# Perceiver block: normalizing attention outputs two head groups at a time, with the softmax sums copied beside them by DMA

## The chip, the cores and the metric

One NeuronCore of one Trainium2 chip runs the whole program. The metric is the device time of one execution in microseconds (us). All times below come from timed runs or from one profiled execution.

## The reference, cut to what matters

The input is `x` (4 batches of 256 tokens, width 256) and a context of 4096 rows of width 192 for each batch. All is float32.

```python
x = x + xattn(layernorm(x), ctx)      # 16 heads of 16; 256 queries, 4096 keys per batch
x = x + attn(layernorm(x))            # 16 heads; keys within 32 positions of the query
x = x + ffn(layernorm(x))             # 16 banks of 256 -> 1024 -> 256, the best 2 of each token
# in both attentions, per head:
out = softmax(q @ k.T / 4) @ v        # then all heads side by side, @ w_out + b_out
```

The softmax is computed as `exp(score - max)`, weighed with `[v, 1]`, and divided by its sum only afterwards. That last division, and how its operands reach their places, is what is changed.

## The kernel before

**Cross-attention (first stage).** Heads go in groups of four (`GH`), so 4 batches give `GROUPS = 16` groups. Each group has `KT = 32` steps, one for 128 keys; there are `STEPS = 512` steps. In step n TensorE (PE) computes the scores of the step (`scores`, L721), the products from which the row maxima of a step 36 later are taken (`max_pair`, L691), and the weighing of an earlier step (`weigh`, L739). ScalarE (ACT) takes the exponential of each step (`empty`, L1242). VectorE (DVE) takes two maxima from PSUM a step (`max_one`, L1494). Between these lie side jobs, written out by `side_jobs(n)`: keys ("kk"), values ("v"), the maxima as rows ("neg"), "norm" and "out". Each side job takes its turn on two pairs of PSUM banks with the scores (`bank_pair`).

`weigh` leaves in PSUM, for head j of the group, rows 32j to 32j+15 of output and row 32j+16 with the softmax sum. ACT copies the 128 x 256 tile to `o_raw` (`ocopy`, L1289). The job "norm", at step 6 of the next group, is a PE matmul of `o_raw` with the selector `lsel` (L747), which puts each head's sum on its rows. ACT copies the result to `total` (L1278), DVE makes a first guess of 1/total by its bits (`guess`, L1517, at step 8), and GpSimd (POOL) refines it three times and multiplies it onto `o_raw` (`norm`, L2040 to L2048). `close_up` (SyncE's queue, SP, at step 17, `CLOSE_AT`) then copies the 16 rows of each head into `o_close`, 128 rows without gaps, by four DMAs. After four groups "out" projects `o_close` (L754, step 22). So there are 15 norm jobs in the loop. The last group is normalized after the loop by `last_norm`: a matmul (L985), a DVE reciprocal (L1523), a product and a sum on DVE.

**Windowed attention (second stage).** Its 16 `PAIRS` run in a PE order written by hand, for i = 1 to 15: `max2(i,0)`, `neg2(i-1)`, `weigh2(i-2,0)`, `scores2(i-1)`, `max2(i,1)`, `weigh2(i-2,1)`, `norm2(i-3)`. After i = 3 follows `last_project` (L900); after i = 5, 6 and 7 the second half of rows, queries, keys and values (`turn_half`, `qk_half`, `v_tile2`), each behind a wait for the exponentials of pair i-1; after i = 8 and 12 `project2` (L880). `norm2` is again an `lsel` matmul (L867); ACT copies its result (`sums2`, L1343), DVE takes the reciprocal (`reciprocals2`, L1554), and POOL multiplies and adds the bias (`norm2`, L2127, L2129). `close_up` again follows. `neg2`, `norm2`, the projections and the logits share one PSUM bank, in the order of `x_uses()`.

**After it.** Routing, then the banks' products on 24 tiles, with 31 loads of weights by DMA. Neither is touched.

Of the kernel before, what the change touches and what calls it, by code (L numbers as in the profile page):

```python
# [16 lines left out]
P = 128  # L17
# [71 lines left out]
CLOSE_AT = 17  # L89
# [68 lines left out]
def side_jobs(n):  # L158
# [38 lines left out]
def weighing():  # L197

    plan, waiting = {}, []
    for n in range(STEPS + 2):  # L200
# [3 lines left out]
        put_off = n < STEPS and len(waiting) < 2 and kinds & {"kk", "v"} and not (kinds & {"neg", "norm"} or after & {"kk", "v"})  # L204
# [18 lines left out]
def x_uses():  # L223

    order = ["norm"]
    for i in range(1, PAIRS):
        order += [("neg2", i - 1)]
        order += [("norm2", i - 3)] if i >= 3 else []
        order += ["out"] if i == 3 else []
        order += [("out2", (i - 8) // NG)] if i in (8, 12) else []  # L230
    order += [("neg2", PAIRS - 1), ("norm2", PAIRS - 3), "logits"]
    return {use: n for n, use in enumerate(order)}
# [24 lines left out]
def build(nc, a, out, scratch):  # L257
    ctx = ExitStack()
    with ctx:
# [8 lines left out]
        def bank(i, n=1):  # L268
# [15 lines left out]
        o_norm = sp_all.tile("o_norm", (NG, SEQ))  # L284
        o_close = sp_all.tile("o_close", (KE, SEQ))
        kept = sp_all.at
# [12 lines left out]
        vals = s1.tile("vals", (KT, HEADS * VW))  # L299
        wts_at = s1.at  # L300
# [13 lines left out]
        total = s1.tile("total", (SEQ,))  # L314
# [10 lines left out]
        bv = s1.tile("bv", (NG,))  # L325
# [49 lines left out]
        bv2 = s2.tile("bv2", (NG,))  # L375
        bo2 = s2.tile("bo2", (EMB,))
        q2 = s2.tile("q2", (2, KE, TOK))
        vals2 = s2.tile("vals2", (TT, HEADS * VW))
        wmask = s2.tile("wmask", (2, WIN))
# [16 lines left out]
        sum2 = [s2.tile(f"sum2_{i}", (SEQ,)) for i in range(2)]  # L396

# [57 lines left out]
        st_qk, pool_lo, ld_o = semaphores("st_qk", "pool_lo", "ld_o")  # L455
# [13 lines left out]
        pe_lastnorm, dve_lastnorm, pe_lastout, dve_lastx = semaphores(  # L469
            "pe_lastnorm", "dve_lastnorm", "pe_lastout", "dve_lastx")  # L470
# [39 lines left out]
        def closed(g):  # L510

            return 16 * GH * (g + 1)
# [38 lines left out]
        def _(e):  # L551
# [216 lines left out]
            def side_job(job):  # L768
# [6 lines left out]
                elif job[0] == "norm":  # L775
                    norm(job[1])
# [98 lines left out]
            def project2(b):  # L875
                e.wait_ge(ld_o, closed(GROUPS + NG * b + NG - 1))
                e.wait_ge(x_free, X_NO["out2", b])
                for qt in range(BT):
                    for k in range(KE):
                        i = e.matmul(bank(X_BANK)[:, qt * EMB:(qt + 1) * EMB], o_close[:, k, qt * P:(qt + 1) * P],  # L880
# [3 lines left out]
            def project_third(qt):  # L884

                if qt == 0:
                    e.wait_ge(ld_o, closed(GROUPS + NG * (BATCH - 1) - 1))
                    e.wait_ge(dve_m2, 2 * PAIRS)
                for k in range(KE):
                    i = e.matmul(bank(W_BANKS[qt])[:, 0:EMB], o_close[:, k, qt * P:(qt + 1) * P], wo2[:, k],  # L890
# [3 lines left out]
            def last_project():  # L894

                e.wait_ge(ld_o, closed(LAST))
# [34 lines left out]
            def early(j):  # L931
                dst = bank(M_BANKS[j % 2])
                if j == 0:
                    e.wait_ge(ld_b, 16 * 8)
# [27 lines left out]
            for n in range(-LEAD, STEPS + 2):  # L962
# [13 lines left out]
                for job in jobs:  # L976
                    if job[0] in ("neg", "norm", "out"):
                        side_job(job)
# [5 lines left out]
            e.wait_ge(act_ocopy, GROUPS)  # L984
            e.matmul(bank(X_BANK)[:, 0:SEQ], lsel, o_raw, start=True, stop=True).then_inc(pe_lastnorm, 1)  # L985
# [33 lines left out]
            for i in range(1, PAIRS):  # L1019
                max2(i, 0)  # L1020
                neg2(i - 1)
                if i >= 2:
                    weigh2(i - 2, 0)
                scores2(i - 1)
                max2(i, 1)
                if i >= 2:
                    weigh2(i - 2, 1)
                if i >= 3:
# [15 lines left out]
                if i in (8, 12):  # L1044
                    project2((i - 8) // NG)
# [1419 lines left out]
```

## Time and profile before

| what | value |
|---|---|
| median of 3 runs | 1208.67 us (1207.93 to 1208.95) |
| profiled execution, its own time | 1209.17 us |
| its span, first to last instruction | 1207.4 us |
| mean granted TensorE clock | 0.986 |
| PE, DVE, ACT, POOL busy | 97%, 71%, 59%, 35% of the span |
| first stage, steps 0 to 511 | 78.6 to about 850.3 us |
| second stage | about 850.3 to about 978 us |

The profiled execution's own time lies 1.8 us over its span and 0.5 us over the median of the runs. Times in the rows are us from the start of the span. Busy time of PE is modelled, so a busy PE is not PE at its peak; what a job costs is read from the distance between the starts of its neighbours.

### The profile page before, as it was taken

How to read it: one execution, taken by the hardware profiler on the slowest of the kernel's cores; microseconds unless marked ns; L12 is line 12 of the kernel's file. 1: busy time of each engine (PE TensorE's matmuls, PEld its weight loads, DVE VectorE, ACT ScalarE, POOL GpSimd, SP SyncE). 2: the span in 40 equal slices, each digit the busy share in tenths (PEclk: the TensorE clock that was granted, in tenths of full speed). 3: DMA queues.
4: the chain of work that ended last, by engine and by line, in shares of the span. 5: the costliest groups of instructions: out<-in, count | busy, mean ns of one | idle time of the engine just before them, and what ended most of it. 6: DMA issues, size and time to landing. Idle time of an engine off the chain costs nothing.

```text
span 1207.4 us, 29836 instructions
## 1 busy us (share of the span) xinstructions
PE 1174.8 (97%) x12106; PEld 721.4 (60%) x12106; DVE 862.5 (71%) x1663; ACT 714.8 (59%) x923; POOL 425.4 (35%) x429
## 2 busy tenths in 40 slices
PE   8989999999999999999999999999899979999998
PEld 5555454566545566655456654444556568778787
DVE  4987899977899987789988789962375774233234
ACT  4437778877787877788777778895233310121120
POOL 3385593225462333554332312212022423222210
PEclk9989999999999999999999999999899998999999
DMA  8766756554575465465644455220300009999993
GB/s 235 111 154 179 188 109 155 122 118 121 129 173 121 110 140 146 122 143 116 148 106 91 102 121 113 56 64 4 89 8 10 11 38 351 413 413 396 390 392 114
DMA packets 62648, 184.78 MB, mean 153 GB/s; under 512 B 19888, under 2 KB 27824, under 8 KB 54576
## 3 DMA queue, kind: packets, MB, share of 16 engines
q1 hardware_dynamic: 58352, 171.27, 51.1%
q0 software_dynamic: 2432, 7.11, 1.8%
q10 hardware_dynamic: 1728, 4.49, 1.0%
q8 instruction: 96, 1.57, 0.6%
q14 instruction: 40, 0.33, 0.1%
HBM read 138.20 MB, written 39.58 MB: 147 GB/s over the span
## 4 chain that ended last, share of the span: by engine, by line
PE 88%; DVE 4%; ACT 2%; DMA 2%; issue 1%; SPq 1%; POOL 1%; ACTq 0%; DVEq 0%; POOLq 0%
PE psum L739 22%; PE psum L721 17%; PE psum L691 10%; PE psum L1152 5%; PE psum L1180 5%; PE psum L589 5%; PE psum L605 4%; PE psum L1177 2%; PE psum L1146 2%; PE psum L802 2%; DVE part_max L1484 1%; ACT wts L1242 1%; PE psum L921 1%; PE psum L796 1%; PE psum L622 1%
## 5 line engine op out<-in xcount | busy, mean ns | idle before, releaser
L1494 DVE TENSOR_REDUCE part_max<-psum 128x1 f32<-128x512 f32 x952 | 600.1, 686 | 98.4 <-PE psum L691 96.7
L1242 ACT ACTIVATE wts<-psum 128x1024 f32<-128x1024 f32 x512 | 518.7, 1024 | 99.4 <-PE psum L721 97.9
L739 PE MATMUL psum<-wts,vals 128*17 128x256 f32 x4096 | 307.2, 384 | 0.5 <-ACT o_raw L1289 0.5
L721 PEld LDWEIGHTS psum<-queries,keys 51*128 51x128 f32 x2048 | 155.8, 185 | 186.3 <-issue 149.6
L721 PE MATMUL psum<-queries,keys 51*128 51x256 f32 x2048 | 255.3, 327 | 2.1 <-ACT queries L1274 0.2
L691 PE MATMUL psum<-keys,queries 51*128 51x512 f32 x1024 | 219.1, 411 | 6.7 <-DVE part_max L1484 2.8
L739 PEld LDWEIGHTS psum<-wts,vals 128*17 128x17 f32 x4096 | 75.1, 96 | 118.7 <-issue 90.3
L691 PEld LDWEIGHTS psum<-keys,queries 51*128 51x128 f32 x1024 | 110.5, 186 | 22.3 <-DVE part_max L1484 10.8
L2040 POOL TENSOR_TENSOR error<-total,o_norm 128x256 f32<-128x256 f32 x45 | 33.0, 734 | 205.8 <-DVE o_norm L1517 203.4
L1414 ACT ACTIVATE hid<-psum,b1s 128x128 f32<-128x128 f32 (+1 forms) x124 | 31.7, 351 | 113.7 <-PE psum L1152 77.3
L1973 POOL CAST key_high<-key_low 128x1024 fp32r<-128x1024 f32 x28 | 29.0, 1036 | 178.0 <-ACT key_low L1255 178.0
L2177 POOL DMA_INDIRECT rows_y<-yout,to_row x22 | 21.7, 987 | 130.0 <-DVE yout L1904 130.0
L1975 POOL TENSOR_TENSOR key_low<-key_low,key_high 128x1024 fp32r<-128x1024 f32 x28 | 66.6, 2380 | 2.3
L1152 PE MATMUL psum<-xTt,w1s 128*128 128x128 f32 x544 | 63.6, 276 | 0.2 <-issue 0.2
L1895 DVE TENSOR_SCALAR hid<-psum,b1s 128x128 f32<-128x128 f32 (+1 forms) x124 | 30.5, 313 | 45.5 <-PE psum L1152 42.4
L1152 PEld LDWEIGHTS psum<-xTt,w1s 128*128 128x128 f32 x544 | 62.2, 192 | 0.5 <-issue 0.4
L1180 PE MATMUL psum<-w2s,hid 128*128 128x256 f32 x272 | 62.1, 382 | 0.0
L1180 PEld LDWEIGHTS psum<-w2s,hid 128*128 128x128 f32 x272 | 50.5, 190 | 11.8 <-issue 5.7
L1988 POOL TENSOR_TENSOR ctx_lo<-ctx_in,ctx_hi 128x1536 fp32r<-128x1536 f32 x16 | 55.7, 3480 | 1.3
L1261 ACT ACTIVATE vals<-psum 128x512 f32<-128x512 f32 x64 | 38.2, 599 | 29.7 <-PE psum L605 16.6
L1533 DVE TENSOR_REDUCE neg_max<-psum 128x4 f32<-128x640 f32 x32 | 26.4, 824 | 38.3 <-PE psum L802 38.3
L1255 ACT ACTIVATE key_low<-psum,bk_two 128x1024 f32<-128x1024 f32 x28 | 31.2, 1115 | 37.4 <-PE psum L589 37.4
(281 smaller groups left out, 1494.1 us busy)
## 6 DMA issues: line engine op xcount, KB each, us to landing
w1s<-in_W SPq DMA_DIRECT2D x31, 1024.0 KB, 10.7
w2s<-in_W SPq DMA_DIRECT2D x31, 1024.0 KB, 11.7
keys<-k_high SPq DMA_DIRECT2D x232, 128.0 KB, 3.9
keys<-k_low SPq DMA_DIRECT2D x116, 128.0 KB, 4.5
k_high<-key_high SPq DMA_DIRECT2D x28, 512.0 KB, 4.9
k_low<-key_low SPq DMA_DIRECT2D x28, 512.0 KB, 3.8
ctx_in<-in_ctxT SPq DMA_DIRECT2D x12, 768.0 KB, 6.5
ctx_in<-in_ctxT ACTq DMA_DIRECT2D x4, 768.0 KB, 12.3
```

The lines of the kernel that those rows point to most:

```text
L589: t = e.matmul(bank(first + odd), w[rows, r, hp * P:(hp + 1) * P], c[rows, p, r * CH:(r + 1) * CH], start=(r == 0 and n == 0), stop=(r == ...
L605: m = e.matmul(bank(first + odd)[:, 0:EMB], c[rows, p, at:at + P], w[rows, r], start=(r == 0 and n == 0), stop=(r == CB - 1 and n == 2))
L691: e.matmul(bank(LEAD_BANKS[m % 2] + i if m < LEAD else M_BANKS[(2 * m + i) % 3]), queries[g % 3][64 * i:64 * i + STK, hh, qt * P:(qt + 1) ...
L721: m = e.matmul(bank(S_BANKS[S_NO["s", n] % 2] + i)[:, hh * SEQ:(hh + 1) * SEQ], keys[64 * i:64 * i + STK, hh, c, at:at + P], queries[g % 3 ...
L739: i = e.matmul(bank(O_BANK)[32 * j:32 * j + VW, 0:SEQ], vals[:, t, h * VW:(h + 1) * VW], wts[n % NW][:, j * SEQ:(j + 1) * SEQ], start=(t = ...
L1152: i = e.matmul(dst[:, q * P:(q + 1) * P], w1s[w[0]][:, k, hc * P:(hc + 1) * P], xTt[j % 2][:, k], start=(k == 0), stop=(k == KE - 1))
L1180: i = e.matmul(dst, hid[j % 2][:, hc], w2s[w[0]][:, hc], start=(hc == 0), stop=(hc == HC - 1))
L1242: i = e.activation(wts[n % NW], s_bank(job, 2), ACT.Exp, scale=QSCALE)
L1261: i = e.activation(vals[:, t:last + 1:CH // P].rearrange("p t (h w) -> p t h w", w=VW)[:, :, :, 0:HD], s_bank(job, 2).rearrange("p (t h w) ...
L1494: e.reduce_max(part_max[g % 2][:, hq, c:c + 1], bank(M_BANKS[n % 3]), AX_X).then_inc(dve_max, 1)
L1975: e.tensor_tensor(key_low, key_f, key_high.bitcast(F32), ALU.subtract).then_inc(split_low, 1)
L1988: e.tensor_tensor(ctx_lo[:, p], ctx_in[:, p], ctx_hi[:, p].bitcast(F32), ALU.subtract).then_inc(pool_lo, 1)
```

## The change

1. The "norm" jobs, `last_norm`, and the `lsel` matmuls of the second stage's first 12 pairs (`WIDE`) are gone, with their ACT copies.
2. `close_up` now copies from the raw outputs, right after ACT has made them (step 2 of the next group): four DMAs for the heads' rows and a fifth one that reads the four rows of sums and writes each 16 times, into `total`, beside the rows it belongs to.
3. Two groups fill the 128 rows of `total` and of one half of `o_close`. DVE's guess and POOL's refinement then run once for two groups, in place on `o_close`, at step 14 (`INVERSE_AT`) of every second group. "out" moves from step 22 to 24. The eighth of these (groups 14 and 15) lies in the second stage.
4. `ocopy` waits for the DMAs of the group before instead of for POOL's product. The weights of the second stage (`ld_b`) are nine loads instead of eight and stand behind `close_up(14)` on SP's queue.
5. The second stage has tiles of its own (`o_close2`, `total2`, `inverse2`). DVE takes one reciprocal for two pairs (`inverse_two`), between its two maxima of i = 5, 7, ... 15. The PE order becomes `max2(i,0)`, `project2`, `neg2(i-1)`, `weigh2(i-2,0)`, `weigh2(i-2,1)`, `max2(i,1)`, `scores2(i-1)`. The last batch's pairs 12 to 15 keep the `lsel` matmuls.

```diff
-CLOSE_AT = 17
+CLOSE_AT, INVERSE_AT = 2, 14
+WIDE = NG * (BATCH - 1)
...
-    if at == 6 and 0 <= g < LAST:
-        jobs.append(("norm", g))
-    if at == 22 and hg == NG - 1 and 0 <= b < BATCH - 1:
+    if at == 24 and hg == NG - 1 and 0 <= b < BATCH - 1:
         jobs.append(("out", b))
...
 # TensorE
-            def norm(g):
-                bank_pair(("norm", g))
-                e.wait_ge(act_ocopy, g + 1)
-                e.matmul(s_bank(("norm", g))[:, 0:SEQ], lsel, o_raw, start=True, stop=True).then_inc(pe_s, 1)
...
             def project(b):
-                e.wait_ge(ld_o, closed(NG * b + NG - 1))
+                e.wait_ge(pool_norm, KE * (b + 1))
...
             def last_project():
-                e.wait_ge(ld_o, closed(LAST))
+                e.wait_ge(pool_norm, GROUPS // 2)
...
-            e.wait_ge(act_ocopy, GROUPS)
-            e.matmul(bank(X_BANK)[:, 0:SEQ], lsel, o_raw, start=True, stop=True).then_inc(pe_lastnorm, 1)
...
             for i in range(1, PAIRS):
                 max2(i, 0)
+                if i in (8, 12):
+                    project2((i - 8) // NG)
                 neg2(i - 1)
                 if i >= 2:
                     weigh2(i - 2, 0)
+                    weigh2(i - 2, 1)
+                max2(i, 1)
                 scores2(i - 1)
-                max2(i, 1)
-                if i >= 2:
-                    weigh2(i - 2, 1)
-                if i >= 3:
+                if i - 3 >= WIDE:
                     norm2(i - 3)
...
 # ScalarE
             def ocopy(g):
                 if g:
-                    e.wait_ge(pool_omul, g)
+                    e.wait_ge(ld_o[(g - 1) % 2], closed(g - 1))
...
             def ocopy2(p):
-                if 1 < p < PAIRS - 1:
-                    e.wait_ge(pool_omul2, p - 1)
+                if 1 < p < WIDE + 2:
+                    e.wait_ge(ld_o[p % 2], closed(GROUPS + p - 2))
+                elif p == WIDE + 2:
+                    e.wait_ge(pool_omul2, inverted(p - 2))
...
                 neg_rows(i - 1)
-                exps(i - 1)
                 if i >= 2:
                     ocopy2(i - 2)
-                if i >= 3:
+                exps(i - 1)
+                if i - 3 >= WIDE:
                     sums2(i - 3)
...
 # VectorE
+            def guess(u):
+                if u:
+                    e.wait_ge(pool_norm, u)
+                for i in range(2):
+                    e.wait_ge(ld_o[i], closed(2 * u + i))
+                e.tensor_scalar(inverse.bitcast(I32), total.bitcast(I32), -1.0, INVERSE_BITS, ALU.mult, ALU.add).then_inc(dve_guess, 1)
...
+            def inverse_two(u):
+                if u:
+                    e.wait_ge(pool_omul2, u)
+                for i in range(2):
+                    e.wait_ge(ld_o[i], closed(GROUPS + 2 * u + i))
+                e.reciprocal(inverse2, total2[u % 2]).then_inc(dve_rec2, 1)
...
-                if n >= KT and n % KT == 8:
-                    guess(n // KT - 1)
+                if n % (2 * KT) == INVERSE_AT and n >= KT:
+                    guess(n // (2 * KT) - 1)
...
                 max2(i, 0)
-                if i >= 4:
-                    reciprocals2(i - 4)
+                if i >= 5 and i % 2:
+                    inverse_two((i - 5) // 2)
+                if i in (8, 12):
+                    add_out2((i - 8) // NG)
                 max2(i, 1)
                 pieces2(i)
+                if i == 1:
+                    guess(GROUPS // 2 - 1)
...
 # GpSimd
+            def norm(u):
+                o = o_close[:, u % KE]
+                e.wait_ge(dve_guess, u + 1)
+                for _ in range(3):
+                    e.tensor_tensor(error, total, inverse, ALU.mult)
+                    e.tensor_scalar(error, error, -1.0, 2.0, ALU.mult, ALU.add)
+                    e.tensor_tensor(inverse, inverse, error, ALU.mult)
+                e.tensor_tensor(o, o, inverse, ALU.mult).then_inc(pool_omul, 1)
+                e.tensor_scalar_add(o, o, bv[:, u % KE:u % KE + 1]).then_inc(pool_norm, 1)
...
+            def norm_two(u):
+                o = o_close2[u // KE % 2][:, u % KE]
+                e.wait_ge(dve_rec2, u + 1)
+                e.tensor_tensor(o, o, inverse2, ALU.mult).then_inc(pool_omul2, 1)
+                e.tensor_scalar_add(o, o, bv2[:, u % KE:u % KE + 1]).then_inc(pool_norm2, 1)
...
 # SyncE's DMA queue
-            def close_up(g):
+            def close_up(g, raw, dst, beside):
                 hg = g % NG
-                if g:
-                    e.wait_ge(ld_o, closed(g - 1))
+                if g > 1:
+                    e.wait_ge(ld_o[g % 2], closed(g - 2))
+                rows = slice(64 * (hg % 2), 64 * (hg % 2) + 64)
                 for j in range(GH):
-                    at = 64 * (hg % 2) + HD * j
-                    e.dma_start(o_close[at:at + HD, hg // 2], o_norm[32 * j:32 * j + HD, hg]).then_inc(ld_o, 16)
+                    e.dma_start(dst[rows.start + HD * j:rows.start + HD * (j + 1), hg // 2],
+                                raw[32 * j:32 * j + HD]).then_inc(ld_o[g % 2], 16)
+                e.dma_start(beside[rows], raw[HD::32].rearrange("p (o t) -> p o t", o=1).broadcast_to([GH, HD, SEQ])).then_inc(ld_o[g % 2], 16)
```

## Rows read from the trace of the kernel before

**Rows 1.** The page: busy us, share of the span and instructions of each engine.
```profile
PE 1174.8 (97%) x12106; PEld 721.4 (60%) x12106; DVE 862.5 (71%) x1663; ACT 714.8 (59%) x923; POOL 425.4 (35%) x429
```
**Rows 2.** Groups of instructions: busy us, mean ns of one, idle before and its releaser.
```profile
L747 PE MATMUL psum<-o_raw,lsel 128*128 128x256 f32 x30 | 10.5, 432 | 0.0
L1517 DVE TENSOR_SCALAR o_norm<-total 128x256 int32<-128x256 int32 x15 | 4.3, 285 | 2.3 <-PE psum L721 2.3
L1554 DVE RECIPROCAL sum<-sum 128x256 f32<-128x256 f32 x14 | 24.4, 1744 | 0.4 <-ACT sum L1343 0.4
```
**Rows 3.** Timeline of PE around one norm job: start us, length us.
```profile
337.31 0.51 PE L721 MATMUL psum<-queries,keys 51*128 51x256 f32 x4
339.19 0.50 PE L721 MATMUL psum<-queries,keys 51*128 51x256 f32 x4
340.41 0.51 PE L721 MATMUL psum<-queries,keys 51*128 51x256 f32 x4
```
**Rows 4.** Timeline of DVE over the same steps.
```profile
339.95 2.51 DVE L1494 TENSOR_REDUCE part_max<-psum 128x1 f32<-128x512 f32 x4 [0.58 <-PE psum L691]
```
**Rows 5.** Timelines of SP's queue and of PE: second stage's loads, their first user.
```profile
799.93 0.34 SPq L2309 DMA_DIRECT2D wqkv<-in_w_qkv  x1
...
815.52 0.66 PE L916 MATMUL psum<-identf,xn 128*128 128x128 f32 x4
```
**Rows 6.** The tile o_close: ns of one issue (min/median/max), us from issue to landing.
```profile
L2259 SPq DMA_DIRECT2D o_close<-o_norm x112: 507/589/1612, 163.0 to 968.0; - x112
...
DMA to landing us min/median/max: 1.7/2.3/4.4
```
**Rows 7.** The chain of waits across the hand-over to the second stage.
```profile
849.32 1.03 PE psum L739 x16
...
851.61 1.77 DVE o_norm L1523
853.52 0.27 PE psum L811 x2
```
**Rows 8.** Windows: length, busy PE, PEld, DVE, ACT, POOL, then PEclk.
```profile
853.70:857.20 3.50, 3.50 (x36) 2.16 (x33) 1.22 (x3) 1.04 (x3) 0.00 (x0) 0.52 0.28 48
...
945.00:982.00 37.00, 31.64 (x371) 20.48 (x370) 29.13 (x67) 10.84 (x23) 14.88 (x19) 1.00 0.07 23
```
**Rows 9.** Timeline of all engines, one iteration (i = 10) of the second stage.
```profile
925.28 0.31 PE L796 MATMUL psum<-wmaskb,identb 128*128 128x160 bf16 x2
926.71 0.29 PE L811 MATMUL psum<-identb,neg_parts 128*128 128x128 bf16 x2
927.33 0.72 PE L830 MATMUL psum<-wmaskb,identb 128*128 128x320 bf16 x4
928.87 0.31 PE L796 MATMUL psum<-wmaskb,identb 128*128 128x160 bf16 x2
928.98 1.30 ACT L1336 ACTIVATE wT<-psum 128x640 f32<-128x640 f32 x2 [1.56 <-PE psum L843]
930.41 0.82 DVE L1533 TENSOR_REDUCE neg_max<-psum 128x4 f32<-128x640 f32 x1 [1.11 <-PE psum L802]
930.70 0.70 PE L867 MATMUL psum<-o_raw,lsel 128*128 128x256 f32 x2
931.29 0.31 PE L796 MATMUL psum<-wmaskb,identb 128*128 128x160 bf16 x2
```
**Rows 10.** Timeline of the second stage: where blocks start, and the last waits.
```profile
873.27 1.10 PE L900 MATMUL psum<-wo,o_close 128*128 128x256 f32 x4 [0.57 <-ACT sum L1343]
...
919.27 0.30 PE L796 MATMUL psum<-wmaskb,identb 128*128 128x160 bf16 x2
...
937.31 0.31 PE L796 MATMUL psum<-wmaskb,identb 128*128 128x160 bf16 x2
...
969.88 1.13 PE L890 MATMUL psum<-wo,o_close 128*128 128x256 f32 x4 [1.71 <-DMA o_close<-o_norm]
...
971.90 1.75 DVE L1554 RECIPROCAL sum<-sum 128x256 f32<-128x256 f32 x1 [0.35 <-ACT sum L1343]
```

More of the change, by code:

```diff
@@ L203, in weighing @@
         after = {job[0] for job in side_jobs(n + 1)} if n + 1 < STEPS else set()
-        put_off = n < STEPS and len(waiting) < 2 and kinds & {"kk", "v"} and not (kinds & {"neg", "norm"} or after & {"kk", "v"})
+        put_off = n < STEPS and len(waiting) < 2 and kinds & {"kk", "v"} and not ("neg" in kinds or after & {"kk", "v"})
         plan[n] = [] if put_off else waiting
@@ L223, in x_uses @@
 def x_uses():
-    order = ["norm"]
+    order = []
     for i in range(1, PAIRS):
+        order += [("out2", (i - 8) // NG)] if i in (8, 12) else []
         order += [("neg2", i - 1)]
-        order += [("norm2", i - 3)] if i >= 3 else []
+        order += [("norm2", i - 3)] if i - 3 >= WIDE else []
         order += ["out"] if i == 3 else []
-        order += [("out2", (i - 8) // NG)] if i in (8, 12) else []
     order += [("neg2", PAIRS - 1), ("norm2", PAIRS - 3), "logits"]
@@ L454, in build @@
         ld_duo = [semaphore(f"ld_duo{i}") for i in range(2)]
-        st_qk, pool_lo, ld_o = semaphores("st_qk", "pool_lo", "ld_o")
+        st_qk, pool_lo = semaphores("st_qk", "pool_lo")
+        ld_o = [semaphore(f"ld_o{i}") for i in range(2)]
         ld_first, pe_first, act_first, dve_firsth, dve_firstl, pool_identb = semaphores(
@@ L976, in _ @@
                 for job in jobs:
-                    if job[0] in ("neg", "norm", "out"):
+                    if job[0] in ("neg", "out"):
                         side_job(job)
@@ L1274, in empty @@
                         i = e.activation(q[at:at + NP].rearrange("p h t -> p (h t)"), src[at:at + NP], ACT.Copy)
-                elif kind == "norm":
-                    if job[1]:
-                        e.wait_ge(pool_omul, job[1])
-                    i = e.activation(total, src[:, 0:SEQ], ACT.Copy)
                 else:
@@ L1302, in _ @@
             e.wait_ge(ld_const, 16)
-            e.activation(total[:, 0:P], identf, ACT.Exp)
+            e.activation(inverse[:, 0:P], identf, ACT.Exp)
             key_ones(slot(4))
@@ L1509, in max_end @@
                 e.wait_ge(dve_negp, g + 1)
-            def guess(g):
-                b, hg = divmod(g, NG)
-                if b:
-                    e.wait_ge(pe_s, done(("out", b - 1)))
-                e.wait_ge(act_s, done(("norm", g)))
-                e.tensor_scalar(o_norm[:, hg].bitcast(I32), total.bitcast(I32), -1.0, INVERSE_BITS, ALU.mult, ALU.add).then_inc(dve_guess, 1)
-            def last_norm():
-                e.wait_ge(pe_s, done(("out", BATCH - 2)))
-                e.wait_ge(pe_lastnorm, 1)
-                e.reciprocal(o_norm[:, NG - 1], bank(X_BANK)[:, 0:SEQ]).then_inc(x_free, 1)
-                e.wait_ge(x_free, X_NO["norm"] + 1)
-                e.tensor_tensor(o_norm[:, NG - 1], o_raw, o_norm[:, NG - 1], ALU.mult).then_inc(own.up(), 1)
-                e.wait_ge(dve_seq, own.n)
-                e.tensor_scalar_add(o_norm[:, NG - 1], o_norm[:, NG - 1], bv[:, NG - 1:NG]).then_inc(dve_lastnorm, 1)
+            def guess(u):
[4 more added lines that the diff above has]
+                e.tensor_scalar(inverse.bitcast(I32), total.bitcast(I32), -1.0, INVERSE_BITS, ALU.mult, ALU.add).then_inc(dve_guess, 1)
             def max2(p, qt):
@@ L1674, in _ @@
             pieces2(0)
-            last_norm()
             last = range((BATCH - 1) * BT, TT)
@@ L2140, in _ @@
                                         ALU.subtract, ALU.mult).then_inc(pool_rows3, 1)
+            for p in range(WIDE, PAIRS - 1):
+                norm2(p)
             for t in (tiles, ends[0], ends[1]):
@@ L2299, in _ @@
                     load_q(e, n // KT + 2)
-                if KT <= n < LAST * KT and n % KT == CLOSE_AT:
-                    e.wait_ge(pool_norm, n // KT)
-                    close_up(n // KT - 1)
+                if n >= KT and n % KT == CLOSE_AT:
+                    g = n // KT - 1
+                    e.wait_ge(act_ocopy, g + 1)
+                    if g > 1 and g % 2 == 0:
+                        e.wait_ge(pool_norm, g // 2)
+                    if g and g % NG == 0:
+                        e.wait_ge(pe_s, done(("out", g // NG - 1)))
+                    close_up(g, o_raw, o_close, total)
             e.wait_ge(pe_s, S_NO["s", LAST * KT])
```

138 lines of the change are left out of this document (65 added, 73 removed).

## The prediction

> **What bounds the kernel now.** I read the page first, then the groups of instructions, then timelines of PE and DVE in the loop and over the second stage, and last the windows with the granted clock. The page shows PE busy for 97% of the span and DVE for 71% [rows 1]. In the loop's plain steps both are full: DVE's maxima follow each other every 2.51 / 4 = 0.63 us, which is 1.26 us for the two of a step [rows 4], and PE's steps start 1.22 to 1.26 us apart [rows 3]. They are tied to each other, for a maximum must leave its bank before PE fills it again. What a step holds beside that lengthens it, and DVE cannot run ahead. The step with the norm job shows this: its scores start at 337.31 and the next ones at 339.19, 1.88 us [rows 3], and DVE then stands idle for 0.58 us [rows 4].
>
> In the second stage PE sets the pace with short waits for DVE and ACT. One iteration takes 931.29 - 925.28 = 6.01 us [rows 9]. By the starts in it `max2` takes 1.43 us, `neg2` and a half of `weigh2` 0.62 (0.22 and 0.40), `scores2` 1.54, `norm2` 0.59. The reader is to see that `norm2` ends at about the time when DVE's maximum does (930.41 + 0.82 = 931.23), and PE's next block waits for that maximum: to take `norm2` out in the old order would give nothing, PE would wait there instead. The new order puts `scores2` behind `max2(i,1)`, so it is the order that makes the gain possible.
>
> **The loop.** 15 norm jobs, two matmul records each [rows 2], stand in it. Each costs 1.88 - 1.26 = 0.62 us of PE's path, so 15 x 0.62 = 9.3 us go. (Busy time alone would say 2 x 432 ns; the starts say what counts.) ACT's copies for them lie inside these 0.62 us. DVE's guess takes 0.285 us [rows 2] and costs something only where DVE is full: eight of the 15 stood in groups without values jobs, four of the new seven do. That is 4 fewer at between 0 and 0.285 us, so 0 to 1.1; I take 0.5. POOL's chain runs half as often, but POOL is busy 35% of the span [rows 1] and its results had slack, so I count nothing; if the cover were gone, a late chain would hold "out". The chain is nine operations and two more, 8 us, started at step 14; "out" at step 24 comes at least 12.5 us later.
>
> What is queued behind the new waits? SP's `close_up` at step 2 stands behind 14 issues of that region (`load_duo` six, `load_q` six, `store_two` two). At 0.589 us each [rows 6] it begins 8.2 us after step 0, its five issues end at 11.2, and at the worst landing of 4.4 us [rows 6] all is there at 15.6. DVE's guess at step 14 comes 14 x 1.26 = 17.6 us after step 0 at the earliest, and keys jobs add to that. The slack of 2 us covers the wait; without it DVE's maxima behind the guess, and so PE, would lose whatever is late. The next `load_duo` (step 8) starts 1 to 2 us late, but its keys are used 12 steps later.
>
> One DMA batch gets later where it shows. The second stage's loads began at 799.93 and their first user on PE ran at 815.52 [rows 5]. Now `close_up(14)` stands before them. It waits for ACT's copy at step 481, about 803.4, and issues five times: the loads begin at 806.4 and are nine. In the old trace data moved for 7.6 us from the first issue, so they land at about 814.0 to 814.5. The user comes at 815.52 - 0.62 = 814.9. So 0 to 2 us are lost; I take 0.3. The loop gives 9.3 + 0.5 - 0.3 = 9.5 us.
>
> **The second stage, up to `last_project`.** The old hand-over: PE ends weighing at 850.35, `last_norm` holds the shared bank, `neg2(0)` starts at 853.52 [rows 7], and PE's clock then stands at 0.52 of full speed for about 3.4 us, and once more at 860.5 [rows 8]. `last_project` starts at 873.27 [rows 10], 22.9 us after the weighing. New: i = 1 is two `max2`, `neg2`, `scores2` and a wait of 0.78 for DVE's first maximum, 5.4 us; i = 2 and 3 are 2 x 1.43 + 0.22 + 2 x 0.40 + 1.54 = 5.42 us each. Sum 16.2 us, so 6.7 us gained; about 3 of them are the clock. `last_project` then starts at about 866.6 in old times. It needs the eighth chain on POOL: five issues from 850.8, landing at about 856.2, then 0.3 of guess and 8 us of POOL, 864.6. DVE waits for that landing in front of the maximum that PE needs at 858.2, so each us of landing past 857 is a us lost; I take 0.3 off.
>
> A rule speaks against the fifth DMA. Its source begins with the four sum rows. The trace of before holds no copy of this shape. The Trainium skill (DMA: Bandwidth & Descriptors, "Why a DMA increments its semaphore by 16 and not by 1") says that a copy uses the largest number of engines up to 16 that divides both slowest dimensions, so this one would run on four, with 16 KB each. At that page's 436 GB/s for all 16 it is an estimate of 0.6 us more, and the sum would be 16.5 instead of 17.1 if all of it came onto PE's path.
>
> **From there to i = 8.** Old: 873.27 to 919.27 [rows 10], 46.0 us. Each of i = 4 to 8 loses 6.01 - 5.42 = 0.59, together 3.0 us. But `scores2` now ends the iteration, and after i = 5, 6, 7 PE waits for both exponentials of that very pair before the second half's blocks. These take 0.11 + 1.30 + 0.05 us from the end of `scores2` [rows 9]; the old order had 2.4 us of other PE work there. This is a new wait of 1.46 us, three times: 4.4 us lost. At i = 4 and 5 DVE's statistics and root stand before the maxima: 0.4 and 0.75 us more than before. At i = 8 `neg2` waits 0.87 for DVE to empty the projection, and 0.56 of waiting for `sums2` goes. Net 3.0 - 4.4 - 1.15 - 0.3 = -2.9 us.
>
> **The rest.** i = 9 to 11: 3 x 0.59 = 1.8 us gained. i = 12 to DVE's last `L1554` reciprocal, 937.31 to 971.90 [rows 10], 34.6 us: new i = 12 is 5.42 + 1.80 + 0.87 = 8.1, i = 13 and 14 are 6.2 each with waits of 0.8 for DVE (statistics, root), and from i = 15 to that reciprocal 11.4 us, since PE's waits for POOL's product and for the last copies, 1.71 us [rows 10], go: 31.9, 2.7 us gained. DVE's reciprocals fall from 14 to 8 of 1.74 us [rows 2]; that lies beside PE and is what keeps the waits this small. Stage two: 6.7 - 0.3 - 2.9 + 1.8 + 2.7 = 8.0; by bounds 3 to 11. I take 7.6, since each wait was placed with exact starts and some will be worse.
>
> Routing and the banks' products only move. Sum: 9.5 + 7.6 = 17.1 us. The profiled execution of 1209.17 becomes 1192.1; it lay 0.5 above the median, so the runs should show 1191.6.
>
> **Rivals.** *The clock stays low in the second stage.* The old drops came behind short waits; the new ones (0.78, and 1.46 three times) are of the size of those at 965 to 970, where the clock stayed full [rows 8]. If two stretches of 3.4 us at half speed come as before, 3.4 us are lost: 1195.0. Chance 0.25. *DVE, not PE, is the loop's pace,* and the norm step's 0.62 us were caught up later: then only 8 us come back, 1201. Against it: DVE idled, and the next steps of 1.22 are no shorter than the others [rows 3, 4]. Chance 0.08. *Slower: the sums land late.* Place: DVE's wait in `guess` and `inverse_two`, 14 of them, with all maxima queued behind. It decides from a landing of about 2 us past my worst of 4.4; each further us costs 7 in the loop and up to 7 later, so at 3.2 us past it the gain is gone, and at 4 the time is near 1218. For it: keys' loads share the queue at step 8. Against it: 112 copies never took over 4.4 [rows 6]. Chance 0.05. *The new waits of the second stage are larger* (exponentials, DVE's order, loads at 814): 3 to 5 us, 1195.5. Chance 0.10. My forecast has the remaining 0.52, between 1189 and 1194.
>
> **Range.** 1187.5 to 1198.5 holds the forecast and the clock and wait cases, and leaves out the caught-up loop, the late landing and an end that is better than all bounds. No change that this kernel's measurement can tell is within 0.2%, 2.4 us. Faster 0.93, same 0.02, slower 0.05.
>
> **What the new profile would show.** No 1.88 us step at step 6 of a group; plain steps still 1.22 to 1.28. The first stage ends near 841, 9.5 us earlier. No `L985`-like matmul and no half clock behind it. In iterations 9 to 11 starts 5.4 us apart. Three PE waits of about 1.5 us for ACT's exponentials before the transposes, the queries' products and the values'. DVE's guesses with no wait for DMA in front. I am wrong if DVE waits on the sums' copies, if the steps grow elsewhere, or if half clock comes back.

## The result and the profile after

Four runs of the changed kernel have a median of 1197.64 us (1187.7 to 1201.35), against 1208.81 us for the kernel before: a ratio of 0.9891 (95% interval 0.9853 to 0.9928). The kernel is faster by 11 us where 17 were forecast. The profiled execution took 1196.13 us (span 1194.3), at a mean granted TensorE clock of 0.986, the same as before (1.00 is 2.4 GHz and 0.50 is 1.2 GHz, the two levels that occur).

The page's first line (busy us, share of the span, instructions) answers [rows 1]:

```profile
PE 1156.3 (97%) x12050; PEld 712.7 (60%) x12050; DVE 848.6 (71%) x1647; ACT 704.9 (59%) x896; POOL 365.4 (31%) x340
```

The first stage first: the timeline of PE at steps 4 to 8 of group 5, to be laid beside [rows 3].

```profile
328.68 0.50 PE L731 MATMUL psum<-queries,keys 51*128 51x256 f32 x4
329.91 0.50 PE L731 MATMUL psum<-queries,keys 51*128 51x256 f32 x4
331.17 0.50 PE L731 MATMUL psum<-queries,keys 51*128 51x256 f32 x4
332.41 0.50 PE L731 MATMUL psum<-queries,keys 51*128 51x256 f32 x4
333.66 0.50 PE L731 MATMUL psum<-queries,keys 51*128 51x256 f32 x4
```

The 1.88 us step is gone: 331.17 to 332.41 is 1.24. The plain steps around it are what they were. From step 0 to the end of weighing the loop took 838.47 - 75.3 = 763.2 us, against 850.35 - 78.6 = 771.75 before: 8.6 us less. (Another 3.3 us came from ahead of step 0. In the old profile PE waits 2.35 us at 29.63 there, and half clock comes at 31; by the same product of keys and queries, 37.80 before and 35.64 now, 2.2 us are there already. Ten further profiles of the changed kernel and its variants start step 0 at 75.2 to 76.5. With one profile of the kernel before, it is not shown whether any of this belongs to the change.)

Then the second stage. The timeline of PE, only blocks with a wait in front, and the two starts that frame i = 4 to 8 (856.44 and 911.77):

```profile
840.84 0.31 PE L798 MATMUL psum<-wmaskb,identb 128*128 128x160 bf16 x2 [0.71 <-DVE neg_max L1518]
...
854.61 1.99 PE L902 MATMUL psum<-wo,o_close 128*128 128x256 f32 x8
856.44 0.30 PE L798 MATMUL psum<-wmaskb,identb 128*128 128x160 bf16 x2
...
859.53 0.31 PE L798 MATMUL psum<-wmaskb,identb 128*128 128x160 bf16 x2 [0.71 <-DVE neg_max L1518]
...
866.22 0.31 PE L798 MATMUL psum<-wmaskb,identb 128*128 128x160 bf16 x2 [1.33 <-DVE neg_max L1518]
866.47 0.54 PE L804 MATMUL psum<-k,q 32*128 32x160 f32 x4
866.94 0.31 PE L798 MATMUL psum<-wmaskb,identb 128*128 128x160 bf16 x2
867.18 0.90 PE L804 MATMUL psum<-k,q 32*128 32x160 f32 x4
...
872.30 1.97 PE L918 MATMUL psum<-identf,xn 128*128 128x128 f32 x8 [1.39 <-ACT wT L1333]
...
884.76 8.56 PE L923 MATMUL psum<-xT,wqkv 128*128 128x512 f32 x16 [1.39 <-ACT wT L1333]
...
900.00 3.72 PE L929 MATMUL psum<-wqkv,xT 128*128 128x256 f32 x16 [1.39 <-ACT wT L1333]
907.92 0.27 PE L813 MATMUL psum<-identb,neg_parts 128*128 128x128 bf16 x2 [0.94 <-DVE x L1576]
...
911.77 0.31 PE L798 MATMUL psum<-wmaskb,identb 128*128 128x160 bf16 x2
...
914.20 0.31 PE L798 MATMUL psum<-wmaskb,identb 128*128 128x160 bf16 x2
...
919.60 0.31 PE L798 MATMUL psum<-wmaskb,identb 128*128 128x160 bf16 x2
```

`last_project` starts 854.61 - 838.47 = 16.1 us after the weighing, where it was 22.9. The iterations from i = 9 on are 919.60 - 914.20 = 5.40 us, where one took 6.01 [rows 9]. The three blocks of the second half each wait 1.39 us for ACT's exponentials. Ahead of them stand waits of 0.71 and 1.33 us for DVE's maxima, at i = 4 and 5. Behind the second of these the same product of keys and queries takes 0.54 us at 866.47 and 0.90 us at 867.18: the clock has fallen, 5 us before the first wait for exponentials ends. The windows (columns as in [rows 8]) show for how long:

```profile
838.50:866.00 27.50, 24.90 (x334) 15.53 (x333) 16.06 (x49) 9.03 (x18) 7.70 (x13) 1.00 0.40 114
866.00:890.00 24.00, 20.99 (x135) 12.00 (x136) 7.88 (x16) 4.56 (x8) 3.02 (x4) 0.57 0.05 12
890.00:945.00 55.00, 50.52 (x624) 31.64 (x622) 30.27 (x71) 18.02 (x36) 7.07 (x9) 1.00 0.07 18
945.00:966.00 21.00, 18.57 (x225) 12.28 (x226) 14.68 (x22) 6.49 (x14) 11.32 (x15) 1.00 0.07 27
```

A mean of 0.57 over 24 us is 24 x 0.43 / 0.5 = 20.6 us at 1.2 GHz, in one piece. At the hand-over, where the old kernel fell to half clock twice, this one stays at 2.4 GHz. So from 856.44 to 911.77 PE needs 55.3 us, where the old kernel needed 919.27 - 875.08 = 44.2 for the same iterations with their `norm2`. What the hand-over and the shorter iterations gave, 6.8 us and 0.6 each, is gone again in this one place: from the end of weighing to the first late reciprocal (961.32) the second stage takes 122.9 us, and took 973.6 - 850.35 = 123.25 before.

Last, SP and DVE at the eighth guess, the only one of 14 uses of the copied sums that waited for its DMA (four copies of rows go ahead of that of the sums):

```profile
838.95 3.04 SPq L2261 DMA_DIRECT2D o_close<-o_raw  x4
842.03 0.60 SPq L2263 DMA_DIRECT2D total<-o_raw  x1
...
845.08 0.29 DVE L1512 TENSOR_SCALAR inverse<-total 128x256 int32<-128x256 int32 x1 [0.99 <-DMA total<-o_raw]
```

### The profile page after: what moved, and what is told of

Its sections match the earlier page's. It is cut to its first block, busy times and chain, and to the rows that moved or that the text cites. A ratio compares the mean times of both kernels' runs of the same rounds, so it can differ in the third digit from the quotient of the medians.

```text
span 1194.3 us, 29561 instructions
## 1 busy us (share of the span) xinstructions
PE 1156.3 (97%) x12050; PEld 712.7 (60%) x12050; DVE 848.6 (71%) x1647; ACT 704.9 (59%) x896; POOL 365.4 (31%) x340
## 3 DMA queue, kind: packets, MB, share of 16 engines
q8 instruction: 96, 1.57, 0.6%
## 4 chain that ended last, share of the span: by engine, by line
PE 84%; DVE 8%; ACT 3%; issue 2%; DMA 1%; SPq 1%; ACTq 0%; POOL 0%; DVEq 0%; POOLq 0%
PE psum L749 20%; PE psum L731 16%; PE psum L701 10%; PE psum L1151 5%; PE psum L1179 5%; PE psum L599 5%; PE psum L615 4%; DVE part_max L1489 3%; PE psum L804 2%; PE psum L1176 2%; PE psum L1145 2%; DVE part_max L1479 1%; PE psum L923 1%; ACT wts L1241 1%; PE psum L798 1%
## 5 line engine op out<-in xcount | busy, mean ns | idle before, releaser
L1409 ACT ACTIVATE hid<-psum,b1s 128x128 f32<-128x128 f32 (+1 forms) x124 | 31.7, 351 | 113.2 <-PE psum L1151 76.8
L1898 DVE COPY yout<-psum 128x256 f32<-128x256 f32 x22 | 9.3, 425 | 56.7 <-PE psum L1179 39.3
```

## The experiments

Ten runs of eight kernels were made in three groups; those of a group shared a chip and its runs of the kernel before. Diffs are against the changed kernel. Each line of the table gives its median over all its executions. The last two columns come from one fit over all 145 executions whose clock is known: one level for each kernel, one slope for all; the changed kernel's level rests on its first four executions too. The slope is 0.99 us (standard error 0.02) for each 0.001 of mean granted clock. "Against the changed kernel" is then the difference in work and waits at one clock, with its 95% bound.

| kernel | executions | median us | ratio to before | mean clock | at clock 0.985, against the changed kernel |
|---|---|---|---|---|---|
| before | 57 | 1210.35 | | 0.985 | +13.9 ± 0.6 |
| changed: again, again2 | 12, 12 | 1203.03, 1199.38 | 0.9954, 0.9912 | 0.978, 0.980 | 0 (level 1195.9) |
| later | 6 | 1194.51 | 0.9869 | 0.983 | -4.0 ± 1.1 |
| fill | 6 | 1190.65 | 0.9878 | 0.989 | +1.0 ± 1.2 |
| oldorder | 12 | 1200.45 | 0.9941 | 0.977 | -1.1 ± 0.8 |
| dummy | 12 | 1211.52 | 1.003 | 0.979 | +10.1 ± 0.8 |
| loads | 6 | 1196.14 | 0.9882 | 0.985 | 0.0 ± 1.1 |
| both | 6 | 1187.95 | 0.9814 | 0.988 | -4.9 ± 1.2 |
| best, best2 | 6, 6 | 1186.4, 1184.18 | 0.9802, 0.9773 | 0.990, 0.992 | -4.8 ± 1.0 |

**again: the changed kernel untouched, for its spread.**

> The changed kernel itself, run more often. Its four runs so far lie between 1187.7 and 1201.35 us with mean granted clocks of 0.991 and 0.980. Theory (the clock): the time falls in line with the mean granted clock, run by run; with 0.990 and more about 1188, with 0.980 about 1201, and the profile of a slow one shows a long stretch of about half clock in the second stage that a fast one lacks. Rival (something else varies, such as DMA landings in the loop): times and clocks are not in line, and the profile shows longer steps in the first stage.

It took 1203.03 us (1193.68 to 1213.72), 0.9954 of before (0.9917 to 0.999). The profile is the first one over again: all three exponential waits, and half clock at the same place for the same time. The first stage is as long (762.6 us, was 763.2), and times and clocks are in line, so the rival falls. Windows:

```profile
838.50:868.00 29.50, 26.32 (x354) 16.23 (x346) 17.02 (x51) 9.02 (x18) 7.75 (x13) 1.00 0.37 107
868.00:889.00 21.00, 18.21 (x125) 10.56 (x125) 5.23 (x12) 4.56 (x8) 3.02 (x4) 0.51 0.05 13
```

**again2: the same on another chip.**

> The changed kernel once more, untouched, as the base line for the three kernels beside it. The 16 executions so far lie at 1188 to 1214 us, and their time falls by about 1.0 us for each 0.001 of mean granted clock; at a clock of 0.99 they stand at about 1190.6, and the kernel before at 1205.1. Expected here: the same two lines, 14 to 15 us apart at one clock, whatever the medians are. If instead the gain at one clock is another on this chip, the clock does not explain the spread.

It took 1199.38 us (1195.32 to 1207.15), 0.9912 of before (0.9889 to 0.9936). Half clock came in the same place, for a little less time: 24 x 0.36 / 0.5 = 17 us, in two pieces. Window:

```profile
866.00:890.00 24.00, 19.88 (x157) 11.07 (x151) 9.25 (x19) 5.19 (x10) 3.01 (x4) 0.64 0.05 13
```

At a clock of 0.99 its own line stands at 1192.1 and that of the kernel before at 1204.5, 12.4 apart, a little under the expected 14 to 15; over all chips it is 13.9 ± 0.6. So the change is worth about 14 us at one clock. The medians show 4.7 to 12 of them because the changed kernel runs at a clock 0.004 to 0.009 lower: on the first chip 0.9776 against 0.9867, which is 9 us.

**later: the second half's blocks one `max2` later,** so that PE has work between `scores2` and them.

```diff
                 max2(i, 0)
+                if i == 6:
+                    e.wait_ge(act_w2, 2 * (i - 1))
+                    for k in range(KE):
+                        turn_half(1, k, bank(k)).then_inc(pe_half, 1)
...
                 scores2(i - 1)
-                if i == 5:
-                    e.wait_ge(act_w2, 2 * i)
-                    for k in range(KE):
-                        turn_half(1, k, bank(k)).then_inc(pe_half, 1)
```

(The queries' and keys' products move from i = 6 to 7 and the values' from 7 to 8 in the same way.)

> The second half's blocks (transposes, query/key products, values) stand behind the first maxima of the next iteration instead of directly behind scores2, so PE has 1.43 us of its own work while ACT takes the two exponentials. Theory (the three waits cost 1.46 us each and give the clock its chance to fall): 4.4 us less at the same clock, so about 1183.5 where the clock stays full, and the half-clock stretch behind them comes less often, so a median of 1184 to 1188. Rival (the waits were hidden by a later wait, for DVE's root or for the maxima): the time at full clock stays at 1188, and the wait turns up before another block.

It took 1194.51 us (1185.85 to 1203.37), 0.9869 of before (0.9821 to 0.9917); at one clock 4.0 ± 1.1 us less, which is the three waits, 3 x 1.39 = 4.2. The median is over the 1184 to 1188 expected. In its profile no block waits for ACT. But half clock came elsewhere, over iterations whose code and waits are those of the changed kernel. Windows:

```profile
843.70:864.00 20.30, 20.30 (x183) 11.50 (x180) 6.84 (x18) 4.13 (x8) 7.49 (x12) 0.50 0.49 143
864.00:945.00 81.00, 76.10 (x890) 47.69 (x882) 45.09 (x111) 26.20 (x52) 9.87 (x13) 0.96 0.07 18
945.00:960.00 15.00, 14.44 (x119) 8.19 (x120) 6.55 (x13) 2.56 (x6) 6.35 (x6) 0.54 0.09 36
```

**fill: work in the waits, which nobody reads.** `keep_busy`, which the kernel has for places behind this stage, is called here too: 7 products of the unit matrix with itself in front of `max2(i,1)` at i = 4 and 5, where PE waits for DVE's maximum, and 13 before each block of the second half.

```diff
                     weigh2(i - 2, 1)
+                if i in (4, 5):
+                    e.wait_ge(act_w2, 2 * (i - 1))
+                    keep_busy(7, 0)
                 max2(i, 1)
...
+                if i in (5, 6, 7):
+                    e.wait_ge(act_ocopy2, i - 1)
+                    keep_busy(13, O_BANK)
                 if i == 5:
```

> The waits of the second stage stay, but PE runs small matmuls of a unit matrix in them: 7 before max2(4,1) and max2(5,1), 13 before each of the three late blocks. They add no work to the path beyond 0.1 to 0.5 us. Theory (the clock falls because PE idles there): full clock in the second stage, about 1188 to 1189 in nearly all runs, a spread under 3 us. Rival (the clock falls for another reason, or the spread is not the clock's): median near 1197 and spread of 10 us as in the changed kernel.

It took 1190.65 us (1188.97 to 1201.56), 0.9878 of before (0.9829 to 0.9927). Its path is no shorter: at one clock it is 1.0 ± 1.2 us above the changed kernel. All of its gain on the same chip, 12 us in the median, is clock, 0.989 against 0.978. The cure is not complete: two of its six executions had a clock of 0.982 and 0.983, and the spread is 12.6 us where under 3 were expected. It fills both kinds of wait at once, so it doesn't tell which of them counts. The windows of the second stage, and the same pair of starts as above:

```profile
837.80:860.00 22.20, 21.20 (x277) 13.38 (x275) 11.74 (x31) 6.97 (x14) 7.73 (x13) 1.00 0.48 136
860.00:900.00 40.00, 36.47 (x382) 23.28 (x386) 18.93 (x43) 11.63 (x23) 4.76 (x6) 1.00 0.06 14
900.00:945.00 45.00, 42.48 (x607) 26.41 (x602) 28.64 (x69) 15.09 (x30) 10.73 (x12) 1.00 0.10 31
```

```profile
855.82 0.30 PE L798 MATMUL psum<-wmaskb,identb 128*128 128x160 bf16 x2
...
870.03 1.09 PE L918 MATMUL psum<-identf,xn 128*128 128x128 f32 x8 [0.56 <-ACT wT L1339]
...
903.40 0.31 PE L798 MATMUL psum<-wmaskb,identb 128*128 128x160 bf16 x2
```

903.40 - 855.82 = 47.6 us, where the changed kernel needed 55.3: half clock cost 7.7 us there. And from the end of weighing to its first late reciprocal (952.9) the stage takes 115.1 us, 8.1 less than the old one.

**oldorder: PE's and ACT's order of before in the second stage,** without the `norm2` jobs.

```diff
                     weigh2(i - 2, 0)
-                    weigh2(i - 2, 1)
-                max2(i, 1)
                 scores2(i - 1)
+                max2(i, 1)
+                if i >= 2:
+                    weigh2(i - 2, 1)
...
+                exps(i - 1)
                 if i >= 2:
                     ocopy2(i - 2)
-                exps(i - 1)
```

> The changed kernel with the old order of the second stage on PE and ACT (scores2 before max2(i,1), the second half of weigh2 last), still without the norm2 matmuls of pairs 0 to 11. Theory (in the old order the matmul lay beside DVE's maximum, so taking it out gives nothing): iterations 9 to 11 are 6.0 us apart, PE waits 0.6 us for DVE's maximum before each max2(i,0); the three waits for exponentials are gone. At full clock 12 x 0.59 - 4.4 = 2.7 us more than the changed kernel, about 1190.5; if the clock stays full more often, its median may still be lower. Rival (the matmul was on the path in either order): iterations of 5.4 us, about 1183.

It took 1200.45 us (1195.46 to 1219.94), 0.9941 of before (0.9908 to 0.9974). An iteration of it, at full clock (timeline of PE):

```profile
904.86 0.31 PE L798 MATMUL psum<-wmaskb,identb 128*128 128x160 bf16 x2 [0.53 <-DVE neg_max L1519]
...
910.88 0.31 PE L798 MATMUL psum<-wmaskb,identb 128*128 128x160 bf16 x2 [0.53 <-DVE neg_max L1519]
```

6.02 us: what `norm2` took is now a wait for DVE, as the prediction read from [rows 9]. So in the old order leaving `norm2` out gives nothing, and 5.40 needs the new order. Yet the whole kernel is 1.1 ± 0.8 us shorter at one clock, where 2.7 more were expected: its blocks of the second half don't wait for ACT. The new order as written pays back all that it gains; `later` keeps the gain without the payment.

Half clock came here too, though PE's waits are short: from 904 to 950 there are five of 0.53 us and one of 0.94. A mean of 0.73 over 38 us is 20.5 us at 1.2 GHz, and the mean clock over its executions, 0.977, is no higher than that of `again`. Window:

```profile
912.00:950.00 38.00, 35.21 (x362) 19.88 (x363) 17.61 (x48) 8.64 (x17) 6.51 (x7) 0.73 0.07 19
```

**dummy: the norm job's product put back, without its bank and its copy.**

```diff
+                if t == 6 and g:
+                    e.wait_ge(act_ocopy, g)
+                    e.matmul(s_bank(("s", n))[:, 0:SEQ], lsel, o_raw, start=True, stop=True)
                 c, at = slot(n // 4), n % 4 * P
```

> Added work: at step 6 of groups 1 to 15 PE runs the old norm job's product (o_raw with the selector, 128 x 256) into the step's own score bank just before the scores, and nobody reads it. The output is not touched. The job's bank turn and ACT's copy stay away. Theory (the norm job cost PE's path): step 6 grows from 1.24 to between 1.67 (the product's busy time of 0.43) and 1.88 (what the old job cost), so the loop is 15 x 0.43 to 15 x 0.62 = 6.5 to 9.3 us longer at the same clock. Rival (DVE is the loop's pace and a longer PE step is caught up): at most 1 us in all, and the steps after the sixth are shorter than 1.24.

1211.52 us (1204.78 to 1221.27), 1.003 of before (0.9998 to 1.0062): 10.1 ± 0.8 us more at one clock, over the 6.5 to 9.3 expected. Timeline of PE in group 5:

```profile
332.74 0.51 PE L734 MATMUL psum<-queries,keys 51*128 51x256 f32 x4
334.02 0.70 PE L730 MATMUL psum<-o_raw,lsel 128*128 128x256 f32 x2
334.64 0.51 PE L734 MATMUL psum<-queries,keys 51*128 51x256 f32 x4
335.88 0.50 PE L734 MATMUL psum<-queries,keys 51*128 51x256 f32 x4
```

The step is 334.64 - 332.74 = 1.90 us, 0.65 over a plain one; in groups 4, 8 and 12, whose step 6 is a longer one, it grows by 0.78. 12 x 0.65 + 3 x 0.78 = 10.1 us, as measured. The steps after it are 1.24, not shorter: nothing is caught up, and the rival (DVE sets the loop's pace) falls. The product alone is the whole price; the old job's copy and bank cost nothing beside it. The lower bound of the expectation was a misreading: 0.43 us is the mean of one of a product's two records, and the two together make the 0.70 us of the row above.

Its second stage is that of the changed kernel, and its profile is a counter-example: half clock for under 4 us, from 874 on, behind the wait of 0.71 us at i = 4. PE being slower there, the wait of 1.33 us at i = 5 did not arise. The three waits for exponentials (884.54, 892.32, 906.15) are there, 1.39 us each, and the clock stays full through all of them. A row of PE and a window:

```profile
884.54 1.09 PE L921 MATMUL psum<-identf,xn 128*128 128x128 f32 x8 [1.39 <-ACT wT L1336]
850.00:950.00 100.00, 91.49 (x1094) 56.33 (x1094) 53.42 (x131) 31.07 (x61) 17.60 (x25) 0.98 0.16 44
```

**loads: the nine loads in front of group 14's copies, as before.**

```diff
+                if n == LAST * KT:
+                    e.wait_ge(pe_s, S_NO["s", LAST * KT])
+                    e.wait_ge(pe_max, 2 * STEPS)
+                    ...
+                        e.dma_start(dst, a[src]).then_inc(ld_b, 16)
                 if n >= KT and n % KT == CLOSE_AT:
```

> One part of the change undone: the nine loads for the second stage are issued at step 480, in front of the sums' and rows' copies of group 14, as before the change, and not behind them. Theory: step 13 of group 15, which took 1.57 us before and 1.85 to 2.51 us in five profiles since, is 1.57 again, so 0.3 to 0.9 us of PE's path come back, 0.6 in the mean; the copies of group 14 land some 5 us later, which nobody needs before the second stage. Rival (the step is longer for another reason, a wait for DVE): no change of step 13.

1196.14 us (1193.68 to 1198.84), 0.9882 of before (0.985 to 0.9915). Step 13 of group 15 is 1.57 us, as forecast. The first product that needs the loads, in the changed kernel and then in this one:

```profile
803.68 0.66 PE L918 MATMUL psum<-identf,xn 128*128 128x128 f32 x4 [0.53 <-DMA bv_last<-in_b_v_last]
```

```profile
802.24 0.66 PE L918 MATMUL psum<-identf,xn 128*128 128x128 f32 x4
```

0.6 us is below what times can tell here (0.0 ± 1.1 at one clock); the step in the profile shows it.

**best: the three edits together,** with products in PE's waits at i = 1, 4, 5, 8, 12, 13 and 14 (9 to 16 of them; the blocks need none any more).

```diff
+                if i == 1:
+                    e.wait_ge(act_s, len(S_JOBS))
+                elif i in (4, 5, 13, 14):
+                    e.wait_ge(act_w2, 2 * (i - 1))
+                if i in (1, 4, 5, 13, 14):
+                    keep_busy(16 if i == 5 else 9, 0)
                 max2(i, 1)
```

> Three edits together on the changed kernel: the second half's blocks one max2 later, so that PE does not wait for the exponentials; the loads of the second stage at step 480; and small products of the unit matrix, read by nobody, where PE waits for DVE in the second stage (i = 1, 4, 5, 8, 12, 13, 14). Theory: at one clock 5.2 us from the blocks and 0.6 from the loads, so 1184.8 us at a clock of 0.99 (1190.6 - 5.8), and the clock is full from the end of the first stage to about 945, so that the mean clock is 0.985 to 0.993 and the median 1182 to 1190. Rival (half clock in the second stage does not depend on what PE does in these waits): stretches of half clock between 840 and 950 as in the kernel with later blocks alone, mean clock 0.98, median 1194.

1186.4 us (1185.73 to 1188.32), 0.9802 of before (0.9771 to 0.9833). Full clock from 838 to 945, as expected; at one clock 4.8 us below the changed kernel instead of 5.8. Windows:

```profile
838.50:866.00 27.50, 26.61 (x368) 16.76 (x356) 14.88 (x48) 8.65 (x17) 7.76 (x13) 1.00 0.39 113
866.00:890.00 24.00, 23.66 (x254) 13.90 (x246) 14.11 (x26) 7.46 (x15) 4.72 (x6) 1.00 0.06 17
890.00:945.00 55.00, 53.42 (x706) 35.11 (x706) 31.55 (x75) 18.92 (x39) 11.62 (x12) 1.00 0.09 27
```

**both and best2: how much of that are the products?** `both` is `best` without them, `best2` is `best` again, on one chip.

> The second half's blocks one max2 later and the loads of the second stage at step 480, without the unit-matrix products. With it, the kernel that has the products too is run again on the same chip, so that the two differ in nothing else. At a clock of 0.985 both stand at 1191.3 us in the runs so far. Theory (products in PE's waits keep the clock): this one has stretches of half clock between 840 and 960, a mean clock of 0.980 to 0.985 and a median of 1191 to 1196, with a wide spread. Rival (the low clock of the kernel with later blocks alone came from that chip or from chance): median and spread as with the products, 1186 to 1189.

> The kernel with all three edits once more (later blocks, earlier loads, unit-matrix products in PE's waits). Theory: as on the other chip, mean clock 0.988 to 0.991, all executions between 1185 and 1189 us, no half clock from the end of the first stage to about 955, and 5 to 9 us below the kernel without the products. Rival: with another chip the half clock comes back in the second stage, and the median lies over 1190.

`both` took 1187.95 us (1185.83 to 1190.23), 0.9814 of before (0.977 to 0.9858); `best2` 1184.18 (1181.49 to 1188.73), 0.9773 (0.9729 to 0.9817). The products are worth 3.8 us, less than the 5 to 9 expected, and at one clock the two kernels are equal (-4.9 and -4.8). Without them the clock in the profile falls once between 838 and 945, after the wait of 1.32 us at i = 5:

```profile
862.00:880.00 18.00, 16.68 (x181) 10.08 (x181) 9.70 (x27) 6.17 (x12) 3.02 (x4) 0.91 0.08 20
```

18 x 0.09 / 0.5 = 3.2 us, and not 20. So the low clock of `later` (0.983 over six executions, `both` 0.988 on the same chip) looks in part like chance, as that rival had it; the two differ in the loads as well. With the later blocks and the earlier loads most of the clock is there, and the products bring the rest.

## Why the prediction was right, and where it was not

The direction and the range held; the single number was 6 us too low. Of its own signs of being wrong two came: half clock came back, and DVE waited for the sums' copies, once, for 0.99 us. Point by point:

- **The norm jobs: right, a little small.** 0.62 us each were forecast; step 6 is 0.63 us shorter in the profile, and the product added by `dummy` cost 0.65 to 0.79. In the profile the loop is 8.6 us shorter, 9.5 were forecast.
- **The guesses: right in size.** A guess at step 10 made a 1.39 us step of a 1.23 one in eight groups before, 1.3 us. Now one at step 16 makes 1.54 in three groups and 1.39 in a fourth, 1.0 us. So 0.3 us and not 0.5.
- **The loads: 0.6 and not 0.3.** Shown by `loads`. Another 0.36 us is in the negative-maximum step of group 13 (3.06, was 2.70), whose cause was not tried.
- **The sums' copies land in time: right.** 13 of 14 uses don't wait. The eighth guess comes 845.08 - 838.47 = 6.6 us after the weighing, where the prediction had 5.85 and a reserve. These 0.8 us lie in the issues: the fifth begins 842.03 - 838.47 = 3.56 us after the weighing, and 0.45 + 4 x 0.589 = 2.8 were forecast. From its start to the guess are 3.05 us, as in the prediction's own sum, which is 0.75 over the median of 2.3 for a 16 KB copy [rows 6]. The Trainium skill's rule in the prediction (DMA: Bandwidth & Descriptors, "Why a DMA increments its semaphore by 16 and not by 1") would by its estimate make such a copy 0.6 us longer; the trace agrees with that in size, but one landing does not show that four engines are the reason. The late guess cost PE nothing in this profile, 0.39 us in that of `again`, whose guess waited 1.43, and 0.31 in that of `again2`.
- **The hand-over: right.** 16.1 us, forecast 16.2, and no half clock in it.
- **i = 4 to 8: the waits right, in size too.** Three waits of 1.39 us (forecast 1.46); 0.71 and 1.33 us for DVE at i = 4 and 5, forecast 0.4 and 0.75 more than before. At full clock (`fill`) the stretch takes 47.6 us against 44.2: 3.4 us lost, forecast 2.9. That the three waits for ACT are the larger part of it is shown by `later`, 4.0 ± 1.1 us.
- **From i = 9 on: right.** 5.40 us an iteration, and 959.64 - 927.98 = 31.7 us from i = 12 to DVE's last `L1547` reciprocal, forecast 31.9.
- **The second stage in sum: right at full clock.** 8.1 us gained in `fill`, 8.0 by the terms, of which the prediction took 7.6.
- **The clock: here the prediction failed.** Its step was the sentence that the new waits "are of the size of those at 965 to 970, where the clock stayed full", with the first rival (two stretches of 3.4 us, 1195.0) at a chance of 0.25. In the profile and in that of `again` there is one stretch of 20.5 us, worth 7.7; in those of `again2` and `loads`, 17 us in two pieces; only in that of `dummy` under 4. Over 28 executions the mean clock is 0.980, where the old kernel has 0.985. The rival had the right mechanism and a third of the length (6.8 us at half clock), so 3.4 us of time against 7.7. The size of a wait was the wrong sign: the old kernel's 1.03 and 1.71 us (965.64 and 969.88) left the clock full, and here it fell behind 0.71 and 1.33. These two are the waits for DVE at i = 4 and 5, which the prediction priced at 0.4 and 0.75 us but did not count among those that could lower the clock.

Add it up: the prediction's 17.1 us held 3 us of clock at the hand-over. The other 14.1 stand against 13.9 ± 0.6 measured at one clock; the profiles' parts, with 3.4 us for the old hand-over's half clock taken off, give 8.6 + 8.1 - 3.4 = 13.3. What the medians lack is clock, and `fill`, which adds nothing but work in the waits, brings most of it back.

What stays open: which of the filled waits keep the clock, those for DVE at i = 4 and 5 or the three for ACT (the clock fell ahead of the three in `again` as here, and stayed full through them in `dummy`); why the clock fell from i = 2 on in `later` and not in the nine other profiles that have the new order, seven of them with the same wait at i = 1; and how much of the difference in mean clock between chips (0.978 and 0.980 for one kernel) is the chip's.

## What to carry to other kernels

Price a change at one clock and the clock by itself: where runs give the granted clock of each execution, a line through time and clock separates them, and here it found 14 us in medians that showed 5 to 12. When a block moves behind the work that feeds it, ask what now stands between it and its producer: the new order saved 0.6 us an iteration and paid 4.2 us in three waits for exponentials that one `max2` put in between would have covered. Short waits in a stage of small matmuls can cost more than their own length, and their size alone does not say which: waits of 0.71 and 1.33 us went before 20 us at half clock, waits of 0.53 did so in `oldorder`, and 1.71 us left it full. Fill them with moved work first, and with products that nobody reads where none is to be had; then judge by the mean clock of many executions.

## What the runs showed of the hardware

- The granted clock stood at 1.2 GHz for 20.5 us behind waits of PE of 0.71 and 1.33 us (859.53 and 866.22), and through the next two of 1.39; in the same stretch of `again` PE was busy for 18.21 of 21 us. With 7 to 13 small bf16 products in these waits it stood at 2.4 GHz (the profile of `fill`), and the mean over the executions was 0.989 instead of 0.978.
- Long waits did not always lower it: in `dummy` it stood at 2.4 GHz through three of 1.39 us, and in the kernel before through 1.03 and 1.71 us. In `oldorder` it stood at 1.2 GHz for 20.5 of 38 us among waits of 0.53 and one of 0.94.
- One stretch of the same code, from i = 2 to `last_project`, ran at 0.50 in one profile and at 1.00 in nine (two of these with products in the wait at i = 1), so a single profile says little of a kernel's clock. By the fit over 145 executions, 0.001 of the mean clock is 0.99 us of this kernel.
- One issue of a copy on SP's queue took 0.60 us (842.03) and 0.76 in the mean of the four ahead of it, and the copy of four rows to 64 partitions, 64 KB, was in use 3.05 us after its issue began.
